# One core, a scan and an attention layer in one program: the orders of the scanning steps made anew, and a chain's eight loads of weights dealt out to the queues of SyncE and ScalarE

## The reference

```
def _L0_cond_ref(x, t_emb, ...):              # d_inner 512, d_state 16
    xr, gate = jnp.split(x @ W_in.T, 2, axis=-1)
    xr = xr + t_emb[:, None, :]
    xc = silu(causal depthwise conv of 4 taps(xr) + b_conv)
    xn = (xc - mu) / jnp.sqrt(var + 1e-05) * ln_g + ln_b
    Bm, Cm, dt = jnp.split(xn @ W_xproj.T, 3, axis=-1)
    dt = jnp.tanh(dt @ W_dt.T + b_dt) * 0.01
    Ad = 1.0 + dt * (-jnp.tanh(A_log))
    Bd = Bm * jnp.minimum(jnp.linalg.norm(xn, axis=-1, keepdims=True), 1.0)
    def step(h, inputs):                      # over the 64 positions
        h = jnp.clip(h * ad[:, :, None] + bd[:, :, None] * xt[:, None, :], -10.0, 10.0)
        yt = jnp.einsum('bd,bdh->bh', ct, h)
    y = ys + D * xn
    return y * silu(gate) @ W_out.T

def _L1_cond_ref(x, ..., styles, num_heads):  # 16 heads of 16
    x = layer norm(x * s1)
    q, k, v = x @ q_weight.T * q_dc, x @ k_weight.T * k_dc, x @ v_weight.T * v_dc * s2
    out = softmax(q k^T / 4) v
    return out @ w_weight.T * w_dc + v @ u_weight.T * u_dc
x = x + _L0_cond_ref(x, cond, ...)
x = x + _L1_cond_ref(x, ..., cond, 16)
```

## Time and profile before

| | us |
|---|---|
| median of three runs | 1810.15 |
| lowest, highest | 1808.18, 1811.61 |
| the profiled execution, its time | 1813.53 |
| its span, first to last instruction | 1811.8 |
| TensorE busy (share of the span) | 1594.8 (88%) |
| VectorE busy | 1402.2 (77%) |
| GpSimd busy | 1196.3 (66%) |
| ScalarE busy | 1136.2 (63%) |
| 16 scans a step on VectorE (L1704), 1008 of them | 812.0, 806 ns each |

### The profile page before, as it was taken

How to read it: one execution, slowest core, us unless ns; L and a number is a source line. 1 busy time by engine, 2 the same in 40 slices (tenths; PEclk the granted TensorE clock), 3 DMA queues, 4 the chain that set the end, 5 groups by cost and what they waited for, 6 DMA issues and landing times. The chain is left out here.

```text
span 1811.8 us, 41467 instructions
## 1 busy us (share of the span) xinstructions
PE 1594.8 (88%) x12460; PEld 1036.9 (57%) x12460; DVE 1402.2 (77%) x2354; ACT 1136.2 (63%) x2913; POOL 1196.3 (66%) x1849
## 2 busy tenths in 40 slices
PE   5438688999999999999999999999899999989886
PEld 5423245666656565656665665656566665546664
DVE  1758677888878888888888788888888888778542
ACT  5664455767667676767676666667676666333552
POOL 0576577787777778777877777777777778323231
PEclk8667789999999999999999999999999999999997
DMA  4135565465555556655665655665556656445220
GB/s 105 45 89 116 113 144 134 121 141 143 130 140 140 133 145 148 148 136 128 140 143 129 142 136 135 145 152 134 140 126 138 150 131 153 114 112 125 66 65 24
DMA packets 223116, 226.37 MB, mean 125 GB/s; under 512 B 53488, under 2 KB 179056, under 8 KB 222896
## 3 DMA queue, kind: packets, MB, share of 16 engines
q1 hardware_dynamic: 222896, 223.71, 51.8%
HBM read 152.45 MB, written 71.17 MB: 123 GB/s over the span
## 5 line engine op out<-in xcount | busy, mean ns | idle before, releaser
L1704 DVE CUSTOM_DVE_ANT_0 gc<-ps_u,gc,hi 128x512 f32<-128x512 f32 x1008 | 812.0, 806 | 75.0 <-issue 2.2
L985 PE MATMUL ps_y<-gc,cms 128*32 128x512 f32 x2048 | 286.4, 632 | 0.3 <-DVE gc L1704 0.2
L970 PE MATMUL ps_u<-xs_sb,stage 64*128 64x512 bf16 x1024 | 201.2, 435 | 69.8 <-issue 51.5
L1286 ACT ACTIVATE a_tap<-a_xr,conv_w 128x128 f32<-128x128 f32 x768 | 244.2, 398 | 8.6 <-DVE a_xr L1636 8.6
L1303 ACT ACTIVATE a_z<-ps,a_nb,a_rs 128x512 f32<-128x512 f32 x64 | 49.7, 777 | 183.1 <-POOL a_nb L583 183.1
L1051 PEld LDWEIGHTS ps<-c_zT,L1T 128*128 128x128 f32 x1024 | 121.2, 194 | 70.9 <-issue 70.6
L550 POOL TENSOR_TENSOR a_tap<-a_tap 128x512 f32<-128x512 f32 x116 | 147.7, 1275 | 16.1 <-ACT a_tap L1286 16.1
L970 PEld LDWEIGHTS ps_u<-xs_sb,stage 64*128 64x128 bf16 x1024 | 76.7, 186 | 137.0 <-issue 92.7
L1051 PE MATMUL ps<-c_zT,L1T 128*128 128x128 f32 x1024 | 130.7, 281 | 24.3 <-DVE c_o L1788 21.0
L923 PE MATMUL ps<-a_xT,WinT 128*128 128x128 f32 x1024 | 139.3, 294 | 10.4 <-ACT a_xT L1276 9.4
L923 PEld LDWEIGHTS ps<-a_xT,WinT 128*128 128x128 f32 x1024 | 133.2, 210 | 16.5 <-ACT a_xT L1276 10.1
(11 more groups left out here) (180 smaller groups left out, 3555.3 us busy)
## 6 DMA issues: line engine op xcount, KB each, us to landing
xs_sb<-xn_parts SPq DMA_DIRECT2D x256, 192.0 KB
xn_parts<-a_parts SPq DMA_DIRECT2D x128, 192.0 KB, 3.0
skip_d_xn<-a_dx SPq DMA_DIRECT2D x64, 256.0 KB, 2.2
xs_sb<-xn_parts SPq DMA_DIRECT2D x128, 128.0 KB
scan_out<-y_sb SPq DMA_DIRECT2D x256, 64.0 KB
c_dx<-skip_d_xn SPq DMA_DIRECT2D x64, 256.0 KB, 6.0
c_y<-scan_out SPq DMA_DIRECT2D x64, 256.0 KB, 5.5
c_wu<-style_rows SPq DMA_DIRECT2D x128, 128.0 KB, 4.3
```

Of the source, the lines that this page charges most:

```text
L970: pe.matmul(ps_u[r][t % 2][:, :], weights[:, :, l * SPAN + 2 * t + r], xs_sb[rows, sig % 2, t, :], start=True, stop=True).then_inc(s[f"b_u ...
L985: pe.matmul(ps_y[quad:quad + 32, :], cms[:, sig % 2, v, r, 32 * u:32 * (u + 1)], gc[r][:, (2 * u + v) % RING, :], start=(u == 0), stop=(u ...
L1286: ins = act.activation(a_tap[:, tap, m, :].rearrange("p (r t) -> p r t", r=2), a_xr[:, m, :, tap:tap + S], ACT.Identity, bias=bias, scale= ...
L1704: dve._custom_dve(bass.dve_ops.TENSOR_ADD_SAT, out=gc[r][:, t % RING, :], in0=ps_u[r][t % 2][:, :], in1=before, s0=hi[:, c % 4, col:col + ...
```

## The change

It has two parts. First, the orders of `second_step`, `step` and `late_step` are new on TensorE, VectorE, ScalarE and GpSimd, and so are the banks. Second, of the eight loads of a chain's weights SyncE issues those with even numbers and ScalarE, in a new function `load_w_half` with the same waits, those with odd numbers; both add to the same semaphore. SyncE's half also moves behind load_dx and load_y. Nothing is added to or taken from the work, and SyncE's order is otherwise as it was.

```diff
-                for k in range(SEQS):
+                for k in range(0, SEQS, 2):
                     sp.dma_start(Wb[k:2 * ROWS:SEQS, c % 2, k, :],
...
                 if chain_due(i, 1) is not None:
                     store_b(chain_due(i, 1))
-                    load_w(chain_due(i, 1))
                 load_dx(c0 + 1)
                 load_y(c0 + 1)
+                if chain_due(i, 1) is not None:
+                    load_w(chain_due(i, 1))
...
+            def load_w_half(c):
+                act.wait_ge(s["b_bst"], 48 * (c + 1))
+                if c < 2:
+                    act.wait_ge(s["w_zero"], 4)
+                else:
+                    for r in range(2):
+                        act.wait_ge(s[f"b_u{r}"], STEPS * (HEAD + SLICES * (c - 1)))
+                for k in range(1, SEQS, 2):
+                    act.dma_start(Wb[k:2 * ROWS:SEQS, c % 2, k, :],
...
```

The full step on ScalarE, as it is now (the other engines' lists change in the same way):

```diff
             def step(i):
...
+                c_exp(c0 - 2, 1)
+                c_exp(c0 - 2, 0)
+                if chain_due(i, 1) is not None:
+                    load_w_half(chain_due(i, 1))
+                c_take_ygT(c0, bank[2])
...
+                a_take_tap(i, 2)
+                a_tanh(i - 1)
                 c_normalise(c0 - 1)
...
                 a_square_sum(i - 2)
```

And a piece of TensorE's and of GpSimd's, the latter around a_dx and c_out:

```diff
             def step(i):
                 a_project_bc(i - 3, 2)
+                a_transpose_x(i, 1)
+                c_weigh_v(c0 - 3, 0)
                 c_transpose_z(c0 - 2, 1)
                 scan_block(sig, 0)
...
+                a_half(i - 1, 0)
+                a_sum(i - 1)
+                c_style(c0)
+                c_final(c0 - 3)
+                a_norm_root(i - 2)
+                a_skip(i - 2)
+                c_var(c0)
```

More of the change, by code:

```diff
@@ L1459, in second_step @@
                 sig = i - SCAN_LAG
-                b_take_y(sig - 1)
-                a_take_xT(i, bank[0])
-                a_take_tap(i - 1, 0)
-                a_take_tap(i - 1, 3)
-                a_take_tap(i - 1, 1)
-                a_second_part(i - 3)
-                a_normalise(i - 2, bank[0])
+                a_take_tap(i - 1, 1)
+                a_take_tap(i - 1, 0)
+                a_take_xT(i, bank[0])
+                a_second_part(i - 3)
+                a_take_tap(i - 1, 3)
+                b_take_y(sig - 1)
@@ L1467, in second_step @@
+                a_normalise(i - 2, bank[0])
+                if chain_due(i, 1) is not None:
+                    load_w_half(chain_due(i, 1))
+                a_take_bcT(i - 3, bank[2])
+                a_first_part(i - 2)
+                a_square_sum(i - 2)
+                a_tanh(i - 1)
                 a_take_tap(i, 2)
-                a_first_part(i - 2)
-                a_tanh(i - 1)
-                a_square_sum(i - 2)
-                a_take_bcT(i - 3, bank[1])
             def step(i):
@@ L1474, in step @@
                 sig, c0 = i - SCAN_LAG, i - C_LAG
-                c_take_xT(c0, bank[0])
+                a_take_xT(i, bank[1])
+                c_take_zT(c0 - 2, bank[1])
+                b_take_y(sig - 1)
+                c_take_oT(c0 - 3, bank[2])
+                c_take_xT(c0, bank[1])
+                c_block_keys(c0 - 2, bank[0])
                 a_take_tap(i - 1, 1)
-                b_take_y(sig - 1)
-                a_take_xT(i, bank[2])
-                c_take_zT(c0 - 2, bank[1])
+                a_take_tap(i - 1, 3)
@@ L1491, in step @@
-                c_block_values(c0 - 2, bank[0])
-                a_square_sum(i - 2)
-                c_exp(c0 - 2, 0)
-                a_take_bcT(i - 3, bank[0])
-                c_exp(c0 - 2, 1)
-                c_take_pT(c0 - 2, 0, bank[1])
-                c_take_pT(c0 - 2, 1, bank[0])
-                a_tanh(i - 1)
-                a_take_tap(i, 2)
+                c_double_v(c0 - 2)
+                c_exp(c0 - 2, 1)
+                c_exp(c0 - 2, 0)
+                if chain_due(i, 1) is not None:
+                    load_w_half(chain_due(i, 1))
@@ L1501, in late_step @@
+                c_take_ygT(c0, bank[2])
+                c_take_pT(c0 - 2, 1, bank[1])
+                c_block_values(c0 - 2, bank[0])
+                a_first_part(i - 2)
+                a_take_bcT(i - 3, bank[1])
+                c_take_pT(c0 - 2, 0, bank[0])
+                a_take_tap(i, 2)
+                a_tanh(i - 1)
+                c_normalise(c0 - 1)
+                a_square_sum(i - 2)
             def late_step(i):
                 sig, c0 = i - SCAN_LAG, i - C_LAG
-                c_take_xT(c0, bank[2])
+                c_take_xT(c0, bank[0])
@@ L1504, in late_step @@
+                c_take_zT(c0 - 2, bank[1])
                 b_take_y(sig - 1)
-                c_take_zT(c0 - 2, bank[0])
                 c_tanh(c0, bank[1])
                 c_take_oT(c0 - 3, bank[2])
-                c_block_keys(c0 - 2, bank[2])
+                c_block_keys(c0 - 2, bank[0])
+                c_take_ygT(c0, bank[2])
                 c_double_v(c0 - 2)
+                if chain_due(i, 1) is not None:
+                    load_w_half(chain_due(i, 1))
                 c_normalise(c0 - 1)
-                c_take_ygT(c0, bank[1])
@@ L1814, in second_step @@
                 sig = i - SCAN_LAG
+                if chain_due(i, 1) is not None:
+                    prepare(chain_due(i, 1))
                 a_silu(i - 2)
+                a_bound_norm(i - 3)
                 scan_step(sig, 0, 0)
@@ L1819, in second_step @@
                 scan_step(sig, 1, 1)
-                a_bound_norm(i - 3)
-                if chain_due(i, 1) is not None:
-                    prepare(chain_due(i, 1))
+                a_stats(i - 2, bank[0])
+                a_take_bc(i - 3, bank[2])
+                a_mean_var(i - 2)
                 scan_step(sig, 2, 0)
@@ L1833, in second_step @@
                 scan_step(sig, 5, 1)
-                a_add_style(i, bank[2])
+                a_add_style(i, bank[1])
                 scan_step(sig, 6, 0)
@@ L1911, in late_step @@
                 scan_step(sig, 7, 1)
-                c_residual(c0, bank[1])
             def last_step(i):
```

176 lines of the change are left out of this document (81 added, 95 removed).

## The result

The changed kernel takes 1850.2 us (median of 4, 1846.6 to 1854.3) against 1810.9 for the kernel before in the same comparison: 2.1% slower, ratio 1.0213, 95% interval 1.018 to 1.0247. The forecast was 1844 in a range of 1799 to 1870. The trace is of a further and slower execution: its span is 1856.7, where the four timed ones have spans of 1844.8 to 1852.6. It is 44.9 over the 1811.8 of before, while the medians differ by 39.3.

A forecast was written before the change was run, and what follows sets the result against it. TensorE was taken as the bound in plain steps (busy 23.23 of 23.98 us). The terms -7 + 48 + 1 - 9 = +33 on a span of 1811.8 gave 1844.8, forecast as 1844 against the median, range 1799 to 1870.

The forecast's parts named there:

- Plain steps: Two of every four steps, preparing and beginning no chain: from 23.98 to 23.7 us each, 24 of them, -7.
- a_dx and the raw loads: On SyncE, a_dx made at +1.3 of the next step, so raw issued at +1.9 (before -1.3), landing at +5.4.
- TensorE's loss ahead of block 1: VectorE waits 2.8 us for raw, its fourth scan ends at +10.0, and TensorE loses about 2.6; not setting the end.
- The step of preparation: Third of four steps, preparing the next chain: 30.9 us against 27.2 before, 13 of them, +48.
- The clock: TensorE's clock falls behind an idle time as often as before, in another step: 0; if every time, +7.
- ScalarE's issues: ScalarE's four weight loads ahead of c_take_ygT take 2.1 us, bounds 0 and 4.2.
- rival (b): Load issues cost ScalarE nothing: step that prepares a chain 28.8, sum +6, 1816 us; chance 0.10.
- rival (c): SyncE's and ScalarE's queues take turns, ScalarE's four loads take 4.2: +27 more, 1871 us; chance 0.12.
- (a): Raw in time because a_dx is made early enough: step that prepares a chain 27.8, about 1798 us; chance 0.16.
- (d): The change does what it says, weights' waits go and nothing takes their place: -69, 1741 us; chance 0.04.
- Ends: Before and behind the full steps: -6 at the last chain's preparation, -3 at the start; bounds 0 and -13 together.
- the 12 steps that begin a chain: The step right behind each preparation becomes plain, 23.7 against 23.57 at full clock before: 12 x 0.1 = +1.

## Why the prediction was right, point by point

- *Plain steps.* Predicted 23.7, measured 23.72. The wait for a_xT is there (0.28 for 0.26 predicted); TensorE does not wait for c_yg in a plain step, where I had 0.2, and TensorE is busy 0.2 more than before, which happens to fill it: there the number is luck.
- *a_dx and the raw loads.* The mechanism is shown by moving a_skip alone. I put raw's issue at +1.9 and it came at +2.7; landing +6.3 against +5.4. The later links came where I had put them: b_parts +15.2 (+15.35), loads +21.1 (+21.4), projection +24.4 (+24.1), 7.05 behind it against 6.8. In part that is two errors that cancel: raw was 0.8 late, and from raw to the loads it took 18.35 where I had 19.5. TensorE's loss ahead of block 1 was 2.0 in step 1210.81 (0.61 and 1.35) and not 2.6, and, as I said, did not set the end.
- *The step of preparation* was the mis-sized term: 30.9 predicted, 31.4 measured at best and 32.4 on the mean. 0.5 is the two small errors at the projection's two ends. The rest is 388.30 - 12 x 31.4 = 11.5 us. 7.0 of it lies behind the start of the projection in four steps (those that start at 791.99, 896.10, 1002.02 and 1519.12), in which the clock fell behind the wait for c_ygT: there 8.1 to 9.6 pass between it and the next step instead of 7.05. The other 4.5 is a queue chain that ended later, half of it in steps 896.10 and 1002.02 (projection at +25.2 and +25.8). The chain does not hang on the clock: step 1416.56 had 1.00 throughout and took 31.39, step 1210.81 had 6.8 us at half and took 31.48. In the latter ScalarE reached its loads only as b_parts landed (c_e at 1231.65), by chance of the slower clock, so there two causes are equally late.
- *The clock.* I took it as moved at no cost, with +7 as the bound. In the steps that begin a chain it no longer falls, which gave back 8.5 us in the 11 and 1.3 in step 16. It fell instead in 11 of the 12 preparations: in ten ahead of the wait for c_ygT, where it cost next to nothing, and in four (three of them for the second time) behind it, for the 7.0.
- *ScalarE's issues.* Predicted 2.1, bounds 0 and 4.2, measured 2.5. That they are not free rules out rival (b): with b_parts long landed (the kernel with its early stores) the four loads alone kept c_ygT back by 1.6. That ScalarE's four took 2.5 and not 4.2 rules out rival (c) as forecast, though not that the queues get in each other's way (below).
- *Rivals (a) and (d)* fall with raw's issue at +2.7. The Trainium skill's rule that issuing engines are not separate queues (DMA: Bandwidth & Descriptors, "Issuing engines are not separate DMA queues") holds as far as the runs show: what two queues save is 4.21 - 2.9 = 1.3 us of issuing, and the split alone gained 0.7%, most of it where the clock no longer fell at the start of a chain.
- *Ends.* Predicted -9. Behind the last of the 12 preparations -5.8, as forecast (-6). Ahead of step 16 it was +4.5 and not -3; the first preparation in it, counted with the others in the forecast, went from 26.97 to 32.84, so the start proper gave 1.4.

Sum on the traces: predicted +33, measured +44.9. The plain steps gave -6.3 (-7 predicted), the 13 preparations +68.1 (+48), the 12 steps that begin a chain -9.8 (+1), the ends -7.2 (-9). So the cause and the sign are as forecast, and the size came out near since two terms that were 20 too low and 11 too high make up for each other in part. The medians, 39.3 apart, lie nearer to the forecast than the traces; that is the one slower execution and no merit. Not tried: whether the a_xT wait of 0.28 can be had away, and how long a load itself takes when the other queue is silent.

## What to carry to other kernels

A store that waits at the head of an in-order queue delays what stands behind it by nearly the full wait (with dx early raw went 4.8 us sooner and the weights 4.3): before moving work, follow each queue from the instruction that waits to the last one whose result is needed, and look at where the producer of the first (here a_skip on GpSimd) went. A DMA issued from a compute engine takes that engine's time and its place in order: put it behind the copies that others wait for, or leave it where it was. Where a queue chain and a fallen clock are late by the same amount, removing one shows little; read a step in which the clock held.
